# Another order of VectorE's and GpSimd's work in the slots of a gated delta rule

## What is computed

```python
q, k, v = (x @ Wq.T, x @ Wk.T, x @ Wv.T)            # each through a causal convolution with 4 taps
g = log_sigmoid(x @ Wg.T); beta = sigmoid(x @ Wb.T)
k = k / norm(k); q = q * 64 ** -0.5
def step(S, (q_t, k_t, v_t, g_t, b_t)):             # over the tokens, per head
    delta = v_t k_t^T - (S k_t) k_t^T
    S = exp(g_t) * S + b_t * delta
    return S, S q_t
```

## Time and profile before

| what | value |
|---|---|
| runs | 1883.1, 1889.06, 1895.6 us |
| the profiled execution's own time | 1890.86 us |
| its span | 1888.9 us |
| VectorE busy in the span | 1302.2 us (69%) |
| TensorE busy (matmul) | 1621.4 us (86%) |
| GpSimd busy | 1068.5 us (57%) |
| steady delta slots (from L615 at 184.2 to L615 at 1193.4) | 56 slots in 1009.2 us |

### The profile page before, as it was taken

How to read it: one execution, slowest core, us unless ns; L and a number is a source line. 1 busy time by engine, 2 the same in 40 slices (tenths; PEclk the granted TensorE clock), 3 DMA queues, 4 the chain that set the end, 5 groups by cost and what they waited for, 6 DMA issues and landing times. The chain is left out here.

```text
span 1888.9 us, 72945 instructions
## 1 busy us (share of the span) xinstructions
PE 1621.4 (86%) x31244; PEld 1239.6 (66%) x31244; DVE 1302.2 (69%) x3029; ACT 669.4 (35%) x1290; POOL 1068.5 (57%) x1261
## 2 busy tenths in 40 slices
PE   7479999999999999999999999776999995798950
PEld 6236666666666666666666666665888885787840
DVE  1388999999999999999899999623555553222214
ACT  1244444444444444444444444211111211233313
POOL 0155565565565565655556556412777776577853
PEclk9799999999999999999999999988999998899985
DMA  6245555555555546555545545425554551699557
GB/s 264 84 83 108 109 110 119 120 111 117 123 107 122 121 102 122 113 109 115 122 109 110 118 111 106 89 53 178 165 172 148 173 149 52 186 252 224 95 93 234
DMA packets 530210, 245.39 MB, mean 130 GB/s; under 512 B 423504, under 2 KB 497872, under 8 KB 528992
## 3 DMA queue, kind: packets, MB, share of 16 engines
q1 hardware_dynamic: 443872, 204.95, 43.5%
q0 software_dynamic: 18432, 18.99, 5.8%
q10 hardware_dynamic: 67584, 16.79, 4.0%
HBM read 169.29 MB, written 71.37 MB: 127 GB/s over the span
## 5 line engine op out<-in xcount | busy, mean ns | idle before, releaser
L373 PE MATMUL delta_p_j<-delta_xt,delta_w 128*128 128x512 f32 x768 | 389.2, 630 | 30.0 <-DMA delta_xt<-in_xt 17.4
L572 DVE SCALAR_TENSOR_TENSOR delta_kq<-delta_hist,cw,delta_kq 128x512 f32<-128x512 f32 x384 | 367.6, 957 | 32.6 <-ACT delta_kq L718 23.6
L711 ACT ACTIVATE delta_hist<-delta_p_j 128x512 f32<-128x512 f32 x192 | 114.9, 599 | 473.2 <-PE delta_p_j L373 464.9
L373 PEld LDWEIGHTS delta_p_j<-delta_xt,delta_w 128*128 128x128 f32 x768 | 132.5, 192 | 145.8 <-issue 112.3
L1220 POOL DMA_INDIRECT slot_tokens<-mix_tokens,mix_slot x192 | 189.9, 989 | 62.4 <-issue 61.8
L860 POOL TENSOR_TENSOR delta_sd<-state,eg_end 128x256 f32<-128x256 f32 x128 | 104.9, 820 | 203.1 <-DVE state L652 203.1
L586 DVE SCALAR_TENSOR_TENSOR delta_yv<-delta_hist,cw,delta_yv 128x512 f32<-128x512 f32 x128 | 166.3, 1299 | 7.5 <-ACT delta_yv L718 5.3
L434 PEld LDWEIGHTS delta_p_i<-delta_kkq,rt 64*64 64x64 f32 x4096 | 130.5, 135 | 59.1 <-issue 44.0
L492 PEld LDWEIGHTS delta_p_c<-delta_r,delta_kkq 64*64 64x64 f32 x2048 | 70.9, 136 | 125.1 <-DVE delta_r L644 71.3
L1343 DVE SCALAR_TENSOR_TENSOR expert_gate<-expert_gate,expert_p_h 88x256 f32<-88x256 f32 x64 | 26.7, 417 | 176.9 <-ACT expert_gate L1363 176.9
L434 PE MATMUL delta_p_i<-delta_kkq,rt 64*64 64x32 f32 (+1 forms) x4096 | 141.6, 213 | 4.5 <-DVE delta_kkq L636 3.8
(11 more groups left out here) (145 smaller groups left out, 3699.5 us busy)
## 6 DMA issues: line engine op xcount, KB each, us to landing
delta_xd<-x_scratch SPq DMA_DIRECT2D x256, 128.0 KB, 4.4
delta_w<-in_wqkv SPq DMA_DIRECT2D x64, 416.0 KB
w<-in_w SPq DMA_DIRECT2D x64, 352.0 KB
delta_eg<-eg_rows SPq DMA_DIRECT2D x128, 130.0 KB
n_scratch<-delta_kkq ACTq DMA_DIRECT2D x128, 128.0 KB
mix_ot<-ot SPq DMA_DIRECT2D x16, 1024.0 KB, 5.7
w<-in_w SPq DMA_DIRECT2D x64, 176.0 KB
ot<-delta_o SPq DMA_DIRECT2D x32, 256.0 KB
```

The source lines that it names most:

```text
L373: mm = pe.matmul(p_j[:, :], w[e][:, (ch * 3 + n) * 128:(ch * 3 + n) * 128 + 128], xt[m // 8 % 2][:, ch * 512:ch * 512 + 512], start=ch == ...
L572: ve.scalar_tensor_tensor(out, view(hist[e], i * 2 * 518 + tap, (259, 2), (1, 256)), cw[:, column:column + 1], out, ALU.mult, ALU.add).the ...
L711: ac.activation(view(hist[e], n * 518 + 3, (259, 2), (1, 256)), p_j[:, :], ACT.Copy)
```

## The change

Three things are moved. In VectorE's program the substitution no longer has rows ahead of the residual of chunk two: all its rows stand behind the sums of squares, a first part before the reciprocal and the rest right after it (rows 0 to 2 and 3 to 6 in odd slots, 7 to 9 and 10 to 14 in even ones, where it was 0 to 1 and 2 to 5, and 6 to 8, 9 to 10 and 11 to 14). The residual of chunk two stands between the first tap of k's convolution and the two others. In GpSimd's program the power becomes the slot's last instruction; the scaling of values that uses it moves to the next slot, behind the decay of chunk one and the off-diagonal part, and the copy into the history moves behind it.

```diff
@@ -558,11 +558,11 @@
 
         @block.vector
         def _(ve):
-            def conv(m, i, tapped, done):
+            def conv(m, i, tapped, done, taps=(2, 1, 0)):
 
                 e = m % 2
                 out = view(kq[e], i * 512, (256, 2), (1, 256))
-                for tap in (2, 1, 0):
+                for tap in taps:
                     if tap == 2:
                         ve.wait_ge(tapped, m + 1)
                         ve.wait_ge(carried, m + 1)
@@ -665,26 +665,26 @@
                 if is_macro(before):
                     conv(before, 1, tap_q, conv_q)
                     gate(before)
-                if even:
-                    substitute(subst_group, range(6, 9))
                 if one:
                     update(*one)
                 if is_macro(m):
-                    conv(m, 0, tap_k, conv_k)
-                if even:
-                    substitute(subst_group, range(9, 11))
-                if odd:
-                    substitute(subst_group, range(0, 2))
+                    conv(m, 0, tap_k, conv_k, (2,))
                 if two_:
                     residual(*two_)
+                if is_macro(m):
+                    conv(m, 0, tap_k, conv_k, (1, 0))
                 if is_macro(before):
                     lengths(before)
                 if even:
-                    substitute(subst_group, range(11, SUB - 1))
+                    substitute(subst_group, range(7, 10))
                 if odd:
-                    substitute(subst_group, range(2, 6))
+                    substitute(subst_group, range(0, 3))
                 if is_macro(before):
                     inverse_lengths(before)
+                if even:
+                    substitute(subst_group, range(10, SUB - 1))
+                if odd:
+                    substitute(subst_group, range(3, 7))
                 if is_macro(mi):
                     horner(mi, rx_done, 16, y1_out)
                 if two_:
@@ -847,8 +847,12 @@
                 po.tensor_tensor(view(kpv, ring(m), (C, 8), (1, C)), view(kpv, ring(m), (C, 8), (1, C)),
                                  view(fk, 0, (1, 8), (0, C)), ALU.mult).then_inc(kp_out, 1)
 
+            def roots(m):
+                if m >= 1:
+                    po.wait_ge(vp_out, m)
+                po.tensor_tensor(root[:, :], n2[:, :], view(s.half_power, 0, (0, 8)), ALU.pow).then_inc(small, 1)
+
             def scale_values(m):
-                po.tensor_tensor(root[:, :], n2[:, :], view(s.half_power, 0, (0, 8)), ALU.pow).then_inc(small, 1)
                 po.wait_ge(small, m + 1)
                 po.tensor_tensor(view(kpv, ring(m) + 512, (C, 8), (1, C)), view(kpv, ring(m) + 512, (C, 8), (1, C)),
                                  view(root, 0, (1, 8), (0, C)), ALU.mult).then_inc(vp_out, 1)
@@ -865,12 +869,14 @@
             for t in range(SLOTS):
                 m, before, mi = t, t - 1, inverse_macro(t)
                 one, two_ = chain_step(t, 0), chain_step(t, 1)
-                if is_macro(m):
-                    carry_in(m)
                 if one:
                     decay_state(*one)
                 if is_macro(mi):
                     off_diagonal(mi)
+                if is_macro(t - 2):
+                    scale_values(t - 2)
+                if is_macro(m):
+                    carry_in(m)
                 if is_macro(before):
                     carry_out(before)
                 if t % 2 and 0 <= (t - 3) // 2 < NG:
@@ -885,7 +891,7 @@
                     factors(before)
                     weight(before)
                     scale_keys(before)
-                    scale_values(before)
+                    roots(before)
 
 
 def expert_weights(sp, a, s, e):
```

## The result

The changed kernel takes 2032.55 us in the median (2029.61 to 2035.06, 4 runs), the kernel before beside it 1892.33 us (1883.1 to 1896.96, 4 runs): a ratio of 1.0747 (95% interval 1.0699 to 1.0795). The change makes the kernel 140 us slower. The forecast was 1988, with a range from 1915 to 2025: the direction holds and so does the loop behind it, the size does not.

What follows compares the result with a forecast made beforehand. The loop between TensorE and VectorE was to become the bound: 19.3 + 18.7 + 1.5 = 39.5 us a pair of slots against 36.04, 3.5 us x 28 pairs = +98 us, median about 1988 us, range 1915 to 2025.

Steps and rivals of the forecast that it cites:

- the loop behind it: TensorE's leg plus VectorE's leg, carrying one slot into the next: from 15.3 us to 19.3 and 18.7, over the 18.02 slot.
- The even slot: Loop in even slots: TensorE's leg 8.65 us plus VectorE's 10.6 us, 19.3 us.
- The wait of VectorE: VectorE reaches the residual of chunk two before TensorE's product is there and idles 1.9 us in every slot.
- The collisions: Substitution instructions beside GpSimd's weights and scaling of keys lose 1.6 us a slot, bounds 0 and 2.1.
- rival (c): GpSimd's power also blocks VectorE's substitution and taps for v: 1.4 us more a slot, time 2068 us, chance 0.03.
- Rival (b): No collision on the substitution, loop as forecast: 36.25 us a pair, +6 us, 1895, up to 1910; chance 0.10.
- its rule, duration less 0.23: A substitution instruction beside a GpSimd instruction loses that one's duration less 0.23 us; 1.04 us costs 0.8.
- The odd slot: Loop in odd slots: legs 8.65 and 10.0 us, 18.7 us, plus 1.5 us of waiting for the inverse.
- the way through memory: From last substitution to `inverse_r` in odd slots, 11.2 to 11.9 us: TensorE waits 1.0 to 1.7, taken as 1.5.
- One sign that the prediction gave: In the changed kernel's profile, the wait of `inverse_r` for its transfer grows in odd slots.
- Outside the steady slots: The first seven slots (no recurrence) and last seven (no projection) were put at 0, within 10 us.
- The rival that VectorE's relief wins: VectorE's shorter work, 0.75 us a slot or up to 0.9, makes the kernel faster: 1838 to 1850 us, chance 0.12.

Runs made afterwards that it cites:

- e6: The changed kernel with GpSimd's scaling of the keys done twice, so its results are not the kernel's: 2193.18 us, 1.163 of the kernel before.
- e13: The changed kernel with filler matmuls on TensorE: 8 (even) and 6 (odd slots) before the y1 wait, 5 before the odd inverse wait: 2011.94 us, ratio 1.0653.
- e14: The kernel before with reciprocal one row earlier, GpSimd's next off-diagonal part and values behind the keys, power last, one substitution row moved to odd slots: 1869.21 us, 0.9893.
- e5: The changed kernel with filler matmuls on TensorE only before the wait for y1, 12 in even and 8 in odd slots: 2049.77 us, ratio 1.0798.
- e4: The changed kernel with the reciprocal put back behind all rows of the substitution: 2009.1 us, 1.0657 of the kernel before.
- e9: The changed kernel with filler matmuls on TensorE: 8 (even) and 6 (odd slots) before the y1 wait, 9 before the odd inverse wait: 2025.83 us, ratio 1.0699.

## Why the prediction was right in direction and short in size

The loop it spoke of is there. In the timeline of the changed kernel, one even and one odd slot on VectorE (`y2`, the residual of chunk two, `y2`; the odd slot's are shown above):

```profile
753.83 0.41 DVE L636 TENSOR_TENSOR delta_kkq<-delta_xd,delta_p_i 128x256 f32<-128x256 f32 x1
...
762.99 0.42 DVE L644 TENSOR_TENSOR delta_r<-delta_kpv,delta_p_c 128x256 f32<-128x256 f32 x1 [2.15 <-PE delta_p_c L467]
...
773.08 0.41 DVE L636 TENSOR_TENSOR delta_kkq<-delta_xd,delta_p_i 128x256 f32<-128x256 f32 x1
```

and on TensorE (last product, chain state of chunk one, `inverse_r`, the last rows of the chain state of chunk two, `inverse_ry1`, and then last product, chain state, projection of k and `inverse_r` of the odd slot):

```profile
754.30 1.05 PE L434 MATMUL delta_p_i<-delta_kkq,rt 64*64 64x16 f32 x30 [0.33 <-DVE delta_kkq L636]
...
755.15 0.27 PE L467 MATMUL delta_p_c<-state,delta_kqg 64*64 64x64 f32 x2
...
761.57 1.03 PE L434 MATMUL delta_p_i<-delta_xd,noff 64*64 64x48 f32 x30
...
762.68 0.23 PE L467 MATMUL delta_p_c<-state,delta_kqg 64*64 64x64 f32 x2
...
771.19 1.06 PE L434 MATMUL delta_p_i<-delta_kkq,rt 64*64 64x32 f32 x30 [1.98 <-DVE delta_kkq L636]
...
773.82 1.73 PE L434 MATMUL delta_p_i<-delta_kkq,rt 64*64 64x16 f32 x30
...
775.29 0.37 PE L467 MATMUL delta_p_c<-state,delta_kqg 64*64 64x64 f32 x2
...
776.52 3.23 PE L373 MATMUL delta_p_j<-delta_xt,delta_w 128*128 128x512 f32 x4
...
783.50 1.03 PE L434 MATMUL delta_p_i<-delta_xd,noff 64*64 64x48 f32 x30
```

Point by point:

- *The even slot.* Forecast 8.65 + 10.6 = 19.3 us. Here the ends of `y2`, 754.24 and 773.49, are 19.25 apart: TensorE's leg 762.91 - 754.24 = 8.67, VectorE's 773.49 - 762.99 = 10.50; in the mean 19.24. Both legs are right within 0.1 us, with the earlier trace rows as the source.
- *The wait of VectorE.* Forecast 1.9 us in every slot; here 2.15 in the even slot (762.99), which is also the mean, and 2.22 in the odd one (784.91), where the mean is 2.63. The waits view of the steady slots (187 to 1327 us), us in total, times, longest:

```profile
DVE delta_r L644 <- PE delta_p_c L467: 138.9, 78, 4.3
...
PE delta_p_i L434 <- DVE delta_kkq L636: 104.3, 91, 2.0
...
PE delta_p_i L434 <- DMA delta_xd<-x_scratch: 6.1, 5, 2.0
```

- *The collisions.* Forecast 1.6 us a slot; two a slot lose 0.949 - 0.205 = 0.74 each, 1.5. The power blocks none of the instructions beside it, as 224 instructions of at most 0.23 us beside it show, so rival (c) falls. Rival (b) falls with the two rows of 0.94 and 0.97 us. That the price, from a single row beside a shorter instruction, came out so near is in part luck: its rule, duration less 0.23, fails in e6, where one more GpSimd instruction on the heels of the others costs nearly all of its 1.04 us. The Trainium skill has the rule (SBUF — State Buffer, "SBUF: two separate sides") that the one who starts first holds the shared port pair for the whole instruction: the rows for the weights and keys agree with it, those for the power do not.
- *The odd slot.* Forecast 8.65 + 1.5 + 10.0 = 20.15 us; in the mean 21.46. VectorE's leg is right (9.98). The step that failed is the price of TensorE's leg: the prediction took it from the earlier trace rows, which stand at full clock ("from that instruction TensorE works without a wait"), and put only the way through memory on top. 10.15 us were forecast and 11.40 measured, 1.25 x 28 = 35 us. The new order gave TensorE waits that it did not have before, and the prediction had named those waits but kept the clock at 1.00. At the end of the even slot TensorE idles 1.98 us for `y1` (771.19), and soon after it runs slow: the last product takes 1.73 us for the 1.05 of the earlier trace rows, the chain state starts 1.80 after `y2` in place of 0.9, and the projection of k takes 3.23 us where four such matmuls at full clock take 1.98 (at 767.23 in the same trace). e13, at full clock, has a leg of 10.61: so 0.8 us of the 1.25 is the clock, shown by e13 beside the changed kernel, and 0.45 what is left. Of that 0.4 is the inverse's way: in e13 `inverse_r` starts 9.2 us after `y2`, 12.0 after the last row, where the sum had 8.8 (7.3 + 1.5) and 11.7. One sign that the prediction gave did not come: `inverse_r` waits for its transfer 5 times for 6.1 us in the changed kernel, no more than before, since TensorE at low clock comes later than the transfer.
- *Outside the steady slots.* Put at 0, "within 10 us"; measured 2.8 + 8.4 - 3.3 = 8 us. Together: 98 + 35 + 8 = 141 us, and 139 were measured. (The 139 are the growth of the span; the medians are 140 apart.) What the 8.4 us of the last slots are made of was not tested.
- *The rival that VectorE's relief wins* (a) fell for the reason given against it: its 0.7 us a slot of less work turned into idle time. e14 turns a part of such relief into time, with the residual left in its place.

What stays open: what part of the clock's fall goes back to which wait. In the changed kernel's steady slots 25 of the 27 low stretches begin less than 2 us after TensorE had waited 2.0 us for `y1`, the two others after it had waited 1.6 and 2.0 us for the loaded inverse. e5 shows that filling the first wait moves the low stretches to the second. How much of the loss of e4 and e6 is the clock was not tested either.

## What to carry to other kernels

Where two engines hand work to each other once per slot, add up the leg of each between the two handings and compare the sum with the slot: an instruction moved ahead of its data costs nothing only as long as that sum stays below the slot, and everything that now stands behind it is added to the leg. When the sum passes the slot, an engine that was full begins to idle, so ask what its clock does in and after that idle time before pricing its leg with rows at full clock. A short instruction does not lose less to another engine's long one than a long instruction does: here 0.2 us became 0.95, and a tap of 0.75 became 1.36 to 1.41.

## What the runs showed of the hardware

- TensorE's granted clock, 1.00 in the slots before (2.4 GHz), fell to half (1.2 GHz) in the changed kernel, each time just after the engine had waited 1.6 to 2.0 us for `y1` or for the loaded inverse: 167 us of low clock in the 56 steady slots, 7 before, 444 in e6. Filling both waits with matmuls took all of it away (e9, e13), and the kernel that did more work was the faster one.
- GpSimd's power on 128 x 8 values takes 1.66 us, and 2.11 when a tap was under way as it started (58 of 64 in the kernel before). It did not delay VectorE's substitution, whose inputs are both in SBUF: 224 of its instructions stood beside the power alone, the longest 0.23 us.
- GpSimd's weights and scaling of keys, each over 512 elements and about 1.04 us long, delayed a substitution instruction of 0.2 us by 0.74 each; one more such instruction on their heels (e6) lengthened VectorE's leg by 0.93 to 0.98 us.
